# Second layer of a graph network: the embedding term of both halves of a chunk in one set of VectorE instructions, and another order of casts on ScalarE

## The reference, cut to what matters

```
gate = silu(edge_attr @ W1.T + b1) @ W2.T + b2          # made by an earlier stage
adapt_logit = sum(ei * (ej @ adaptW.T), axis=-1)         # 32 products for each edge
gate = gate + adapt_logit
msg  = gate * h[dst] * (cw * mj)[:, None]
agg  = segment_sum(msg, src, num_segments=N)
```

## Time and profile before

| | us |
|---|---|
| runs | 19371.97, 19425.97, 19426.68; median 19425.97 |
| the profiled execution, its own time | 19498.8 |
| its span, first to last instruction | 19497.0 |
| this stage's one-hot instructions, first and last start | 8977.1 and 10472.6 |

### The profile page before, as it was taken

The page is one execution under the profiler, slowest core; times in us unless marked ns, Lnnn a source line. Parts: engine busy times, 40 slices in busy tenths (PEclk is TensorE's granted clock), DMA queues, the critical chain, the costliest instruction groups (busy, mean ns, idle before and its releaser), DMA issues. The chain is left out here.

```text
span 19497.0 us, 597789 instructions
## 1 busy us (share of the span) xinstructions
PE 12039.6 (62%) x200859; PEld 9977.6 (51%) x203067; DVE 12685.6 (65%) x26741; ACT 5081.6 (26%) x14023; POOL 7739.5 (40%) x7745
## 2 busy tenths in 40 slices
PE   5666666666660056676776666666675676666667
PEld 4555555555550035564554545554564465455456
DVE  8555555555552246678997866776686676667666
ACT  0222222222222135502442044124303302311320
POOL 0555555555556624402331055125405613622640
PEclk7888888888875579998888988998895596588569
DMA  7444444444445648787998777777697888878877
GB/s 295 157 156 155 156 155 156 156 156 155 156 148 161 138 154 282 245 280 275 338 331 235 248 258 261 237 268 261 213 305 255 286 270 276 298 252 273 299 255 246
DMA packets 2039788, 4485.05 MB, mean 230 GB/s; under 512 B 383651, under 2 KB 820609, under 8 KB 2038903
## 3 DMA queue, kind: packets, MB, share of 16 engines
q1 hardware_dynamic: 1422358, 3108.06, 50.3%
q0 software_dynamic: 437168, 1034.15, 14.1%
q10 hardware_dynamic: 180144, 341.27, 4.8%
HBM read 2732.28 MB, written 2060.98 MB: 246 GB/s over the span
## 5 line engine op out<-in xcount | busy, mean ns | idle before, releaser
L1412 POOL DMA_INDIRECT messages<-exp_stage,exp_block_rows x2820 | 2992.9, 1061 | 5357.6 <-ACT exp_stage L1393 2403.5
L817 POOL DMA_INDIRECT records<-rec,row_i x3125 | 2992.0, 957 | 2868.1 <-DVE rec L683 2105.2
L1513 PE MATMUL sum_sums<-sum_slots,sum_onehot 128*128 128x48 bf16 (+1 forms) x94752 | 2728.4, 183 | 947.3 <-DVE h L1477 700.0
L1513 PEld LDWEIGHTS sum_sums<-sum_slots,sum_onehot 128*128 128x128 bf16 x94752 | 2569.5, 96 | 1227.8 <-issue 1226.3
L1278 PE MATMUL exp_rows<-tab,h 128*128 x13536 | 1843.8, 313 | 1214.3 <-issue 596.4
L1272 PE MATMUL exp_rows<-tab,h 128*128 x40608 | 1733.4, 194 | 1051.7 <-DVE exp_times L1322 430.3
L1278 PEld LDWEIGHTS exp_rows<-tab,h 128*128 128x128 bf16 x13536 | 1385.3, 136 | 1672.3 <-issue 1667.1
L737 PE MATMUL ps_l<-place,turned 98*128 98x98 f32 x6250 | 1131.3, 346 | 1745.2 <-ACT place L622 1741.2
L737 PEld LDWEIGHTS ps_l<-place,turned 98*128 98x128 f32 x6250 | 1019.1, 250 | 1832.7 <-issue 1832.7
L1272 PEld LDWEIGHTS exp_rows<-tab,h 128*128 128x128 bf16 x40608 | 1589.4, 100 | 500.6 <-issue 296.1
L683 DVE TENSOR_TENSOR rec<-ps_g,emeta 128x240 f32<-128x240 f32 x625 | 254.8, 408 | 2188.0 <-remote 1423.6
(11 more groups left out here) (298 smaller groups left out, 21297.7 us busy)
## 6 DMA issues: line engine op xcount, KB each, us to landing
exp_places<-src_places SPq DMA_DIRECT2D x1692, 512.0 KB
sum_slots<-messages SPq DMA_DIRECT2D x1410, 576.0 KB, 5.2
messages_first<-fill SPq DMA_DIRECT2D x624, 375.5 KB
sum_slots<-messages_back SPq DMA_DIRECT2D x282, 600.0 KB, 5.2
messages_back<-fill ACTq DMA_DIRECT2D x624, 270.8 KB
sum_slots<-messages_first SPq DMA_DIRECT2D x282, 576.0 KB, 5.4
messages<-fill ACTq DMA_DIRECT2D x624, 260.0 KB
l_places<-dst_places SPq DMA_DIRECT2D x282, 512.0 KB
```

The costliest lines, as they stand in the source:

```text
L817: pool.indirect_dma_start(rec_dram, bass.IndirectOffsetOnAxis(ap=row_i[:, g, k:k + 1], axis=0), rec[:, g, k, :], None).then_inc(put[g], 16)
L1412: pool.indirect_dma_start(to_dram, bass.IndirectOffsetOnAxis(ap=row_d[:, c, g:g + 1], axis=0), stage[:, c, g, :], None, bounds_check=last_ ...
L1513: last = pe.matmul(sums[:, c % RS, g, 0:width], onehot[:, c % RS, g * B + k, :], of[:, n * width:(n + 1) * width], start=n == 0, stop=n == ...
```

## The change

VectorE now does `messages` once for a chunk. It takes the products with the embedding for unit 2c and for unit 2c+1 (two instructions, into one buffer twice as large), then one sum, one scaling and one addition for all 16 slots, and then the two final products. ScalarE does in each step t second term of t-1, third term of t-2, then first term of t. The small buffers for the sum and the scaled sum are now slices of two existing tiles. TensorE's, SyncE's and GpSimd's lists and all their waits are as they were. The core of the diff:

```diff
-            uxv = scoped(s4, "l1_uxv", [P, 2, BH, G], F32)
-            logit = scoped(s4, "l1_logit", [P, B], F32)
-            scaled = scoped(s4, "l1_scaled", [P, B], F32)
+            uxv = scoped(s4, "l1_uxv", [P, CH, 2, BH, G], F32)
+            logit, scaled = mean[:, 0:CS], var[:, 0:CS]
...
                         for t in range(RH):
-                            first_term(i, first, t)
                             for d, step in ((1, second_term), (2, third_term)):
...
+                            first_term(i, first, t)
...
-                        dve.wait_ge(l_mm, i * RH + (t + 1))
...
-                        if t or not first:
-                            dve.wait_ge(l_done, i * RH + t)
-                        if t >= NU or not first:
-                            dve.wait_ge(l_third, i * RH + (t + 1 - NU))
-                        dve.tensor_tensor(uxv[:, :, :, :], hvg[:, :, :, MSG:HV], by_group(us[:, q, at, :]),
-                                          ALU.mult).then_inc(l_step, 1)
+                        if c or not first:
+                            dve.wait_ge(l_done, i * RH + 2 * c)
+                        for h in range(2):
+                            t = 2 * c + h
+                            dve.wait_ge(l_mm, i * RH + (t + 1))
+                            dve.tensor_tensor(uxv[:, h, :, :, :], rows_at(t)[:, :, :, MSG:HV],
+                                              by_group(us[:, q, half(h), :]), ALU.mult).then_inc(l_step, 1)
+                        dve.wait_ge(l_step, step(2))
+                        dve.tensor_reduce(logit, uxv[:, :, :, :, :].rearrange("p h a k f -> p (h a k) f"), AX.X,
                                           ALU.add).then_inc(l_step, 1)
...
+                        for h in range(2):
+                            t = 2 * c + h
+                            if t >= NU or not first:
+                                dve.wait_ge(l_third, i * RH + (t + 1 - NU))
+                            dve.tensor_tensor(by_group(left(t)), by_group(gate[:, q, half(h), 0:MSG]),
+                                              rows_at(t)[:, :, :, 0:MSG], ALU.mult).then_inc(l_done, 1)
```

More of the change, by code:

```diff
@@ L1597, in gnn_kernel @@
             hv_flat = hv[:, :, :, :].rearrange("p w j f -> p (w j f)")
-            STEPS = 4
+            STEPS = 5
             with nc.Block() as block:
@@ L1665, in onehots @@
                                           pcol1[:, :], None, ALU.is_equal).then_inc(l_oh, 1)
[L1667 to L1671, removed]
-                        by_group = lambda a: a.rearrange("p (a k) f -> p a k f", a=2)
-                        dve.wait_ge(l_mm, i * RH + (t + 1))
-                        if h == 0:
-                            dve.wait_ge(ldg[q], (i * AGAIN + (c // RS + 1)) * 16)
-                            dve.wait_ge(ldu[q], (i * AGAIN + (c // RS + 1)) * 16)
-                        if t or not first:
-                            dve.wait_ge(l_done, i * RH + t)
-                        if t >= NU or not first:
-                            dve.wait_ge(l_third, i * RH + (t + 1 - NU))
-                        dve.tensor_tensor(uxv[:, :, :, :], hvg[:, :, :, MSG:HV], by_group(us[:, q, at, :]),
-                                          ALU.mult).then_inc(l_step, 1)
-                        dve.wait_ge(l_step, step(1))
-                        dve.tensor_reduce(logit[:, :], uxv[:, :, :, :].rearrange("p a k f -> p (a k) f"), AX.X,
@@ new lines, in messages @@
+                    def messages(i, first, c):
+                        q = c % RS
+                        step = lambda k: i * (RC * STEPS) + (c * STEPS + k)
+                        by_group = lambda a: a.rearrange("p (a k) f -> p a k f", a=2)
+                        half = lambda h: slice(h * HS, (h + 1) * HS)
+                        rows_at = lambda t: ps_hv[:, t % NV, :, 0:BH * HV].rearrange("p a (k f) -> p a k f", k=BH)
+                        dve.wait_ge(ldg[q], (i * AGAIN + (c // RS + 1)) * 16)
+                        dve.wait_ge(ldu[q], (i * AGAIN + (c // RS + 1)) * 16)
+                        if c or not first:
[7 more added lines that the diff above has]
+                        dve.tensor_reduce(logit, uxv[:, :, :, :, :].rearrange("p h a k f -> p (h a k) f"), AX.X,
@@ L1685, in messages @@
                                           ALU.add).then_inc(l_step, 1)
-                        dve.wait_ge(l_step, step(2))
-                        dve.tensor_tensor(scaled[:, :], logit[:, :], gate[:, q, at, D + CW],
-                                          ALU.mult).then_inc(l_step, 1)
                         dve.wait_ge(l_step, step(3))
-                        dve.tensor_tensor(gate[:, q, at, 0:D], gate[:, q, at, 0:D],
-                                          scaled[:, :].unsqueeze(2).to_broadcast([P, HS, D]),
+                        dve.tensor_tensor(scaled, logit, gate[:, q, :, D + CW], ALU.mult).then_inc(l_step, 1)
@@ L1692, in messages @@
+                        dve.wait_ge(l_step, step(4))
+                        dve.tensor_tensor(gate[:, q, :, 0:D], gate[:, q, :, 0:D],
+                                          scaled.unsqueeze(2).to_broadcast([P, CS, D]),
                                           ALU.add).then_inc(l_step, 1)
-                        dve.wait_ge(l_step, step(4))
-                        dve.tensor_tensor(by_group(left(t)), by_group(gate[:, q, at, 0:MSG]),
-                                          hvg[:, :, :, 0:MSG], ALU.mult).then_inc(l_done, 1)
+                        dve.wait_ge(l_step, step(5))
@@ L1699, in turn @@
                             onehots(i, first, c)
[L1700 to L1705, removed]
+                            if c:
+                                messages(i, first, c - 1)
+                            elif not first:
+                                messages(i - 1, False, RC - 1)
                     turns(dve, TURNS, turn)
-                    for t in range(2):
-                        messages(TURNS - 1, False, t - 2 + RH)
+                    messages(TURNS - 1, False, RC - 1)
                 @block.tensor
```

## The result

| | median us | lowest to highest | chunk in the stage |
|---|---|---|---|
| before | 19405.66 | 19371.97 to 19426.68 | 5.32 us |
| changed | 19938.47 | 19907.87 to 19964.27 | 7.10 us |

A forecast was written before the change was run, and what follows sets the result against it. VectorE, 92% busy, was taken to set the pace, DMA engines close behind. Ring 6.11 + 0.57 x 1.58 = 7.01 us; (7.01 - 5.32) x 282 = +477 us on 19426 gives 19903 us, range 19670 to 20050.

The forecast's parts named there:

- The ring: TensorE's refill of `ps_hv` and VectorE's steps follow in turns, since both slots are held to chunk's end: 7.01 us against 5.32.
- VectorE's saving: Merged sum, scaling and addition leave VectorE 4.35 us of its own work a chunk, 0.97 us less, 273 us over 282 chunks.
- The ring at the high level: With TensorE at its high clock, refill 3.11, hand-over 0.04 and VectorE's steps 2.96 us make 6.11 us a chunk.
- The share at the low level: 57% of chunks run with TensorE at its low clock, the middle of two other stages' 22 and 92%.
- my term for the clock: TensorE's low clock level adds 0.57 x 1.58 us to the 6.11 us ring.
- ScalarE's order at nothing: ScalarE's new order of terms costs nothing and is needed, as unit 2c-1's second term would otherwise come late.
- Rival 1: `ps_hv` refill stays hidden, VectorE's 273 us saving counts; DMA share 0.97 holds chunks at 5.16 us, gain 45 us; chance 0.05.

## Why the prediction was right

- **The ring.** Right, shown from two sides: a third slot, or shorter products, and the loss is gone; ScalarE's order alone leaves the time as it was.
- **VectorE's saving.** Right in size (0.686 and 0.959 us for 0.69 and 0.97), and it returned as idle time: 713.5 / 282 = 2.5 us a chunk, against 7.01 - 4.35 = 2.7. VectorE's five steps in the ring take 3.02 us in the mean, for 2.96.
- **The ring at the high level, 6.11 us.** Too long by 0.3: 5.79 was measured at PEclk 1.00. The terms that were off are the subtractions (0.35 us for 0.51) and the second group (1.09 for 1.29), where I added durations with their ends instead of distances between starts.
- **The share at the low level, 57%.** Measured 58 to 60% of the time (0.71 and 0.70). The share on the ring is what counts, and it is greater than that of the time: in the timelines of the changed kernel 53% of the first groups and 75% of the second took over 1.7 us. The clock cost 7.07 - 5.79 = 1.28 us a chunk, against 0.57 x 1.58 = 0.90. The two errors have opposite signs, and the sum, 7.01 against 7.10, was better than its terms: that part was luck. With the right ring at the high level and my term for the clock, the chunk would have come out at 5.79 + 0.90 = 6.69 us and the loss at 386 us instead of 477. The 57% too was the middle of two other stages (22 and 92%) and not a forecast from a mechanism; nothing in the rows before fixed it. The Trainium skill (TensorE: Matmul & The Clock Gate, section A second HAM failure mode: psum-queue depth-cycling) says that a TensorE which idles briefly between groups of matmuls as it cycles through PSUM swings between its two clock levels. The trace agrees: 0.88 before, 0.70 after, and 1.00 with the pause filled.
- **ScalarE's order at nothing.** Right; that it was needed, wrong.
- **Rival 1's hold by the DMA engines**, 5.16 us and 45 us of gain: wrong. The share fell to 0.75 as forecast (0.74), but 4.66 us were reached with all the bytes. Without the hold the rival allowed 273 us; the most that was seen was 161 us, with three slots and two thirds of the products left out.

## What to carry to other kernels

Before merging instructions on a busy engine, ask how long the merged one holds the buffers that feed it. With as many slots as it reads at once, producer and consumer take turns, and the saving turns into idle time; give it one slot more, or leave it split. Here the slot took away the loss and brought next to nothing beyond: the merged list came near to setting the pace (4.66 us against its 4.35) only when TensorE's products were short too. When an engine that was off the path comes onto it, price it at the clock that its new pauses earn, and add up distances between starts, not durations.

## What was not expected of the hardware

Six extra matmuls a chunk in TensorE's pause took 349 us off the kernel (PEclk 0.70 to 1.00). Cutting the products to a third brought TensorE to the low level for the whole stage (0.50, busy 52%). A DMA share of 0.97 was not saturation: it rose to 1.02 while the rate went from 337 to 384 GB/s (and a share above 1.00 shows that this column is no strict share of time). And one chip ran the unchanged kernel in 17421 us, the others in 19343 to 19492, while a chunk of the changed stage took 7.07 us there and 7.10 us elsewhere.
